# Middle attention layer: scores on and above the diagonal only, the other half transposed from their exponentials, edges multiplied in afterwards

## The reference

```python
A = jnp.concatenate([a_0, a_1, a_2, a_3], axis=1)
e = jnp.einsum('bid,bjd,dk->bkij', hidden, hidden, A)
e = jax.nn.leaky_relu(e, negative_slope=LEAKY_SLOPE)
scores = jnp.full_like(e[:, 0], NEG)
scores = jnp.where(adj == 1, e[:, 0], scores)
...
attn = jax.nn.softmax(scores, axis=-1)
return jnp.einsum('bij,bjd->bid', attn, hidden)
```

## Time and profile before

| | |
|---|---|
| median of 3 runs | 1610.05 us (1607.6 to 1613.08) |
| the profiled execution | 1606.74 us |
| its span, first to last instruction | 1604.9 us |
| first stages, until about | 440 us |
| attention stage | the rest |
| instructions | 32666 |

### The profile page before, as it was taken

The page is one execution under the profiler, slowest core; times in us unless marked ns, Lnnn a source line. Parts: engine busy times, 40 slices in busy tenths (PEclk is TensorE's granted clock), DMA queues, the critical chain, the costliest instruction groups (busy, mean ns, idle before and its releaser), DMA issues. The chain is left out here.

```text
span 1604.9 us, 32666 instructions
## 1 busy us (share of the span) xinstructions
PE 1465.7 (91%) x12740; PEld 1268.5 (79%) x12740; DVE 1137.0 (71%) x3198; ACT 921.2 (57%) x1825; POOL 203.2 (13%) x201
## 2 busy tenths in 40 slices
PE   3999998799836979999999999999999999999984
PEld 2999997555425859899898898988989889898774
DVE  3666664688635577887878878878788787886653
ACT  2777876122224666766657667566675766755620
POOL 4434430000000001011010111100111101010000
PEclk9999999799957989999999999999999999999996
DMA  9999991377811212213222132231322313212010
GB/s 189 207 209 213 210 210 67 110 244 244 288 39 47 79 47 69 76 47 99 54 85 81 39 106 76 57 93 28 112 74 54 93 35 105 67 34 61 28 35 25
DMA packets 108446, 161.94 MB, mean 101 GB/s; under 512 B 9344, under 2 KB 59136, under 8 KB 106240
## 3 DMA queue, kind: packets, MB, share of 16 engines
q1 hardware_dynamic: 85248, 117.86, 24.4%
q0 software_dynamic: 18432, 33.56, 11.4%
q10 hardware_dynamic: 4608, 8.39, 1.5%
HBM read 151.40 MB, written 41.94 MB: 120 GB/s over the span
## 5 line engine op out<-in xcount | busy, mean ns | idle before, releaser
L1329 PE MATMUL ps<-hV,wts_B 128*128 128x129 f32 x2048 | 246.2, 276 | 3.2 <-ACT wts_B L1128 3.0
L1329 PE MATMUL ps<-hP_A,wts_A 128*128 128x129 f32 x2048 | 239.0, 277 | 6.1 <-DVE wts_A L884 3.4
L1329 PE MATMUL ps<-hP_C,wts_C 128*128 128x129 f32 x2048 | 239.1, 277 | 6.0 <-DVE wts_C L884 6.0
L1329 PEld LDWEIGHTS ps<-hV,wts_B 128*128 128x128 f32 x2048 | 238.2, 192 | 4.6 <-ACT wts_B L1128 4.3
L1329 PEld LDWEIGHTS ps<-hP_A,wts_A 128*128 128x128 f32 x2048 | 234.4, 193 | 8.6 <-DVE wts_A L884 5.2
L1329 PEld LDWEIGHTS ps<-hP_C,wts_C 128*128 128x128 f32 x2048 | 234.3, 193 | 8.3 <-DVE wts_C L884 5.7
L889 DVE SCALAR_TENSOR_TENSOR wts_B<-wts_B 128x1024 f32<-128x1024 f32 x128 | 153.9, 1221 | 30.2 <-ACT wts_B L1124 30.2
L884 DVE SCALAR_TENSOR_TENSOR wts_A<-row_A,least_A,ring_A 128x1024 f32<-128x1024 f32 x128 | 161.2, 1275 | 9.2 <-ACT row_A L1108 8.3
L1124 ACT COPY wts_B<-ps 128x1024 f32<-128x1024 f32 x128 | 129.4, 1011 | 60.0 <-PE ps L1316 60.0
L884 DVE SCALAR_TENSOR_TENSOR wts_C<-row_C,least_C,ring_C 128x1024 f32<-128x1024 f32 x128 | 162.3, 1274 | 0.8 <-DMA ring_C<-maskT_scratch 0.8
L307 ACT ACTIVATE maskT<-ps 128x1024 fp8e4<-128x1024 bf16 x128 | 131.1, 1024 | 49.7 <-PE ps L341 37.7
(11 more groups left out here) (228 smaller groups left out, 2543.2 us busy)
## 6 DMA issues: line engine op xcount, KB each, us to landing
adj_b<-in_adj POOLq DMA_DIRECT2D x128, 256.0 KB, 9.1
maskT_scratch<-maskT SPq DMA_DIRECT2D x16, 1024.0 KB, 6.9
ring_A<-maskT_scratch SPq DMA_DIRECT2D x64, 256.0 KB, 3.3
off<-maskT_scratch SPq DMA_DIRECT2D x32, 512.0 KB, 6.7
ring_C<-maskT_scratch SPq DMA_DIRECT2D x64, 256.0 KB, 3.1
xa<-in_x SPq DMA_DIRECT2D x16, 512.0 KB, 4.3
whT_scratch<-whT_s ACTq DMA_DIRECT2D x32, 256.0 KB, 6.5
whT_b<-whT_scratch SPq DMA_DIRECT2D x16, 512.0 KB, 4.8
```

The lines of the kernel that those rows point to most:

```text
L1329: last = nc.tensor.matmul(Q_SLOTS[c // 2 % 2][:, c % 2, 0:PW], wts[x][:, j, c * P:c * P + P], src[:, j, :], start=(j == 0), stop=(j == T - 1))
```

## The change

The scores are symmetric, so tile row j is made only from its diagonal tile on (columns 128 j to 1023), without the penalty matmul. Keep, leaky and exponential work on that part alone. PE then transposes the 28 tiles above the diagonal of the exponentials into PSUM (`turn_rows`, 7 + 6 + ... + 1 tiles, in five groups placed between the columns of `weigh("A")`). `lower` on DVE multiplies the transposed tiles of row k by their edges and writes them below the diagonal, as column k of `wts["B"]`; `upper` on POOL multiplies the upper part of row k by its edges in place. The mask `off` is used as it is loaded, in its plain form, and `complement` is gone. `weigh("B")` waits for `up` and `low`. 

Around this, orders are rewritten: in the gram part C's `turn_h` comes first and the other C steps one place earlier; ACT takes two exponentials early and the other six after the last keep; `load_off` waits for `up` and `low` and stands behind the masks of C on SP, `save` behind `load_x`; the two elu steps of DVE move back. The turn i = B (16), which has no A, gets an order of its own: the transposes, then half of `weigh("C")`, all of `weigh("B")`, and the other half of `weigh("C")`.

```diff
-        PEN = 2048.0
...
-        pen_id = sb("pen_id", [P, P], bf16, side="right")
...
-        nc.vector.tensor_scalar(pen_id[:, :], ident[:, :], -PEN / EDGE_VALUE, None, ALU.mult)
...
+LT = T - 1
+GROUPS_T = ((0, 1), (1, 2), (2, 3), (3, 5), (5, 7))
+TURNED = [(1, 0), (0, 0), (1, 0), (0, 0), (0, HALF), (1, 0), (1, HALF)]
+def turned(k):
+    slot, at = TURNED[k]
+    return P_SLOTS[slot][:, at:at + (LT - k) * P]
...
         def load_off(b, h):
             if b > 0:
-                sp.wait_ge(S["B", "gram"], (b - 1) * T + 4 * h + 4)
+                sp.wait_ge(S["B", "up"], b * T)
+                sp.wait_ge(S["B", "low"], b * LT)
             sp.dma_start(off[:, 4 * h:4 * h + 4, :], maskT_dram[b, :, 4 * h:4 * h + 4, :]).then_inc(S["B", "ring"][h], 16)
...
-            if 0 <= i - 3:
-                save(i - 3)
             if 1 <= i + 1 < B:
                 load_mask("A", i + 1, 0)
                 load_mask("A", i + 1, 1)
-            if 0 < i < B:
-                load_off(i, 0)
-                load_off(i, 1)
             if 1 <= i + 2 < B:
                 load_q(i + 2)
             if 0 <= i - 2 < B:
                 load_mask("C", i - 2, 2)
                 load_mask("C", i - 2, 3)
+            if 0 < i < B:
+                load_off(i, 0)
+                load_off(i, 1)
             if 2 <= i + 2 < B:
                 load_x(i + 2)
+            if 0 <= i - 3:
+                save(i - 3)
             if 0 <= i - 1 < B:
                 load_mask("C", i - 1, 0)
                 load_mask("C", i - 1, 1)
...
+        def upper(b, k):
+            if k % 4 == 0:
+                pool.wait_ge(S["B", "ring"][k // 4], (b + 1) * 16)
+            if k < LT:
+                pool.wait_ge(S["B", "turned"], b * LT + k + 1)
+            else:
+                pool.wait_ge(S["B", "exps"], b * T + k + 1)
+            w = wts["B"][:, k, k * P:N]
+            pool.tensor_tensor(w, w, off_fp8[:, k, k * P:N], ALU.mult).then_inc(S["B", "up"], 1)
         for i in range(-1, B + 1):
+            if i >= 1:
+                upper(i - 1, 0)
+                upper(i - 1, 1)
             if i + 1 < B:
                 rstd("A", i + 1)
+            if i >= 1:
+                for k in range(2, T):
+                    upper(i - 1, k)
...
         def leaky(b, j):
             dve.wait_ge(S["B", "kept"], b * T + j + 1)
-            nc.vector.scalar_tensor_tensor(wts["B"][:, j, :], wts["B"][:, j, :], SLOPE, wts["B"][:, j, :], ALU.mult,
-                                           ALU.max).then_inc(S["B", "lrelu"], 1)
-        def complement(b, h):
-            dve.wait_ge(S["B", "ring"][h], (b + 1) * 16)
-            nc.vector.tensor_scalar(off_int[:, 4 * h:4 * h + 4, :], off_int[:, 4 * h:4 * h + 4, :], EDGES, None,
-                                    ALU.bitwise_xor).then_inc(S["B", "off"], 1)
+            w = wts["B"][:, j, j * P:N]
+            nc.vector.scalar_tensor_tensor(w, w, SLOPE, w, ALU.mult, ALU.max).then_inc(S["B", "lrelu"], 1)
+        def lower(b, k):
+            dve.wait_ge(S["B", "turned"], b * LT + k + 1)
+            if k == 0:
+                for h in range(2):
+                    dve.wait_ge(S["B", "ring"][h], (b + 1) * 16)
+            ks = slice(k * P, k * P + P)
+            nc.vector.tensor_tensor(wts["B"][:, k + 1:T, ks], turned(k).rearrange("p (t q) -> p t q", q=P),
+                                    off_fp8[:, k + 1:T, ks], ALU.mult).then_inc(S["B", "low"], 1)
...
+            def elu_positive():
+                dve.wait_ge(S["C", "quo"], (i - 2) * PARTS)
+                nc.vector.scalar_tensor_tensor(old[:, :, :], quo[:, :, :], 0.0, old[:, :, :], ALU.max, ALU.add)
+            def elu_negative():
+                dve.drain()
+                dve.wait_ge(S["C", "quo_exp"], i - 2)
+                nc.vector.scalar_tensor_tensor(old[:, :, :], elu[:, :, :], 1.0, old[:, :, :], ALU.min,
+                                               ALU.add).then_inc(S["C", "done"], 1)
...
@@ -937,30 +976,63 @@
                 leaky(i - 1, 0)
             if post:
                 highest_share("C", 2)
-                dve.wait_ge(S["C", "quo"], (i - 2) * PARTS)
-                nc.vector.scalar_tensor_tensor(old[:, :, :], quo[:, :, :], 0.0, old[:, :, :], ALU.max, ALU.add)
+            if post and not GW:
+                elu_positive()
             if GW:
                 leaky(i - 1, 1)
+            if CA:
+                columns("C", i - 2)
+            if GW:
                 leaky(i - 1, 2)
             if CA:
-                columns("C", i - 2)
+                exponents("C", i - 2)
             if GW:
                 leaky(i - 1, 3)
-            if CA:
-                exponents("C", i - 2)
-            if GW:
                 leaky(i - 1, 4)
             if CA:
                 factors("C", i - 2)
-            if post:
-                dve.drain()
-                dve.wait_ge(S["C", "quo_exp"], i - 2)
-                nc.vector.scalar_tensor_tensor(old[:, :, :], elu[:, :, :], 1.0, old[:, :, :], ALU.min,
-                                               ALU.add).then_inc(S["C", "done"], 1)
             if GW:
                 leaky(i - 1, 5)
                 leaky(i - 1, 6)
                 leaky(i - 1, 7)
+            if post and GW:
+                elu_positive()
+            if i == B:
+                lower(i - 1, 0)
+                weights("C", i - 2, 0)
+                weights("C", i - 2, 1)
+                lower(i - 1, 1)
+                weights("C", i - 2, 2)
+                lower(i - 1, 2)
+                weights("C", i - 2, 3)
+                lower(i - 1, 3)
+                lower(i - 1, 4)
+                elu_negative()
+                weights("C", i - 2, 4)
+                lower(i - 1, 5)
+                lower(i - 1, 6)
+                for j in range(5, T):
+                    weights("C", i - 2, j)
+                shares("C", i - 2, 0)
+                shares("C", i - 2, 1)
+                shares("B", i - 1, 0)
+                shares("B", i - 1, 1)
+                add("B", i - 1, 0, newC, oldC)
+                dve.drain()
+                stats("C", newC, 0)
+                shares("B", i - 1, 2)
+                shares("B", i - 1, 3)
+                highest_share("B", 1)
+                add("B", i - 1, 1, newC, oldC)
+                dve.drain()
+                stats("C", newC, 1)
+                moments("C")
+                shares("C", i - 2, 2)
+                shifts("C", i - 1)
+                return
...
                 dve.wait_ge(S["A", "qT_made"], i + 2)
                 nc.vector.tensor_tensor(newA[:, :, :], newA[:, :, :], TURN_Q.rearrange("p (t d) -> p t d", t=T),
                                         ALU.add).then_inc(S["A", "x1"], 1)
+            if GW:
+                lower(i - 1, 0)
+            if nextA:
                 dve.drain()
                 stats("A", newA, 0)
             if AA:
                 shares("A", i, 0)
+            if GW:
+                lower(i - 1, 1)
             if nextA:
                 stats("A", newA, 1)
                 moments("A")
             if AA:
                 shares("A", i, 1)
+            if GW:
+                lower(i - 1, 2)
             if CA:
                 weights("C", i - 2, 0)
+            if GW:
+                lower(i - 1, 3)
+                lower(i - 1, 4)
             if AA:
                 add("A", i, 0, newB, oldB)
             if nextA:
                 shifts("A", i + 1)
+            if AA:
+                shares("A", i, 2)
+            if GW:
+                lower(i - 1, 5)
+                lower(i - 1, 6)
+            if post and GW:
+                elu_negative()
             if CA:
                 weights("C", i - 2, 1)
-            if AA:
-                shares("A", i, 2)
-            if CA:
                 weights("C", i - 2, 2)
...
                 shares("B", i - 1, 3)
+            if post and not GW:
+                elu_negative()
...
             if j == 0 and b > 0:
                 act.wait_ge(S["B", "tile"], b * T)
-            nc.scalar.copy(wts["B"][:, j, :], P_SLOTS[j % 2]).then_inc(S["B", "kept"], 1)
+            nc.scalar.copy(wts["B"][:, j, j * P:N], P_SLOTS[j % 2][:, j * P:N]).then_inc(S["B", "kept"], 1)
         def score_exps(b, j):
             act.wait_ge(S["B", "lrelu"], b * T + j + 1)
-            nc.scalar.activation(wts["B"][:, j, :], wts["B"][:, j, :], ACT.Exp, bias=shiftB[:, 0:1]).then_inc(S["B", "exps"], 1)
+            w = wts["B"][:, j, j * P:N]
+            nc.scalar.activation(w, w, ACT.Exp, bias=shiftB[:, 0:1]).then_inc(S["B", "exps"], 1)
...
                 scaled("C", i - 3, 3)
+            if CA:
+                relu_hT("C", i - 2, "A", min(i + 1, B))
             if GW:
                 keep_scores(i - 1, 0)
                 keep_scores(i - 1, 1)
+                score_exps(i - 1, 0)
+                score_exps(i - 1, 1)
+                keep_scores(i - 1, 2)
+                keep_scores(i - 1, 3)
             if CA:
```

(94 more changed lines are left out.)

17 lines of the change are left out of this document (6 added, 11 removed).

## The result

The changed kernel takes 1616.29 us (median, 1611.93 to 1620.43), the kernel before beside it 1608.85. The ratio is 1.0045, 95% interval 1.0026 to 1.0063: slower, by about 7 us or 0.45%, where 1591 and a gain of 1% were forecast. The profiled execution took 1615.00 us, its span 1613.2 (1604.9 before).

What follows compares the result with a forecast made beforehand. PE was taken to bound the steady turn: -4.9 + 2.4 + 1.1 = -1.4 us, times 14 = -20; with -3.5 (i = 1) and +5 (end), 1606.7 became 1588, as median 1591; its own range 1578 to 1604, whole range 1560 to 1625.

Steps and rivals of the forecast that it cites:

- PE's sum and the gram chain: Steady turn: PE's own work 4.9 us shorter, 2.4 lost to a chain through the neighbours; gram part 12.0 us, not 17.45.
- rival (e): Narrow matmuls don't shorten as their columns say: together 0.3 us more a turn, inside the range; no chance of its own.
- The A part: Steady turn, PE: weighing 14.3, turn_q 0.87, transposes 3.05, together 18.2 us; the added waits all have cover over 1 us.
- GpSimd's rate: Upper steps on GpSimd: 2.2 ns a column, between bounds 1.45 and 2.9; 10.9 us a turn.
- The contention: Port pair shared by GpSimd and DVE: up 7 late for B's first column, 1.1 us a turn, bounds 0 and 1.9.
- Turn 16: Without an A part to cover the transposes, DVE's list ends at 30.2 and the last turn of C comes 6.2 us later.
- Turn 17: elu_negative leaves the way in front of weights C: -1.2 us.
- i = 1: Gram starts 1.9 us earlier, lasts some 10.6 us instead of 15.3, and transposes add 3.05: -3.5 us.
- (c): Slower by the port pair, GpSimd dear: at 2.9 ns a column up 7 is late, 1630 us; chance 0.27, including no change 0.10.
- (a): No contention: up 7 and shifts A in time, -2.5 us a turn, 1577 us; chance 0.19.
- (d): New waits drop PE's granted clock to 1.2 GHz for a while, adding 3 us a turn: 1633 us; chance 0.05.
- the four signs of being wrong: Gram part of 14 us, upper rows above 2.5 ns a column, granted clock under 0.95, last C turn not late.

## Why the prediction was wrong

**The sign.** -20 - 3.5 + 5 = -18.5 was forecast, the spans say +8.3.

**PE's sum and the gram chain: right.** 12.0 us, measured 12.11. The three stalls named were 0.9 for keep 2, 0.9 for `us_C` and 0.5 near the end; the trace has 0.18, 0.79 and 0.60, the last one on `hP_C` at A's first column, and one of 0.20 on `peak_C` that wasn't named. The chain is the one foreseen; that its sum came out to 0.1 is partly luck. Narrow matmuls cost as their columns say (three of 256 columns start within 0.33 us), so rival (e) is out.

**The A part: right.** 18.2 forecast, 18.38 measured, without a wait of PE in this turn.

**GpSimd's rate: right.** 2.2 ns a column was the middle between 1.45 and 2.9, and 1024 columns took 2.02 us, 2.0 ns a column. Up 7 ended at 938.57, 31.0 us behind the turn's start against 29.4 undisturbed and 33.7 with every claim served in turn. By PE's own pace B's first column reaches row 7 at about 939.6 (938.05 and 14 instructions of 0.112 us, an estimate), so it was in time. That the rate fell near the middle of so wide a pair of bounds is partly luck.

**The contention: right in kind, wrong in place and size; this is the step that failed.** The term is +1.1 us, for B's first column behind GpSimd, with nothing for the rest of the B part. Measured: 0 at the first column, +2.1 in the B part (20.03 against 17.94; up to 2.4 in three turns), nearly all at the values of the next A. The prediction costed GpSimd's own end. GpSimd did lose time (its six steps took 8.11 us, 6.5 forecast undisturbed), but it had cover. VectorE, which stood as well, had not: the earlier trace rows show GpSimd's power waiting for a weights step, and the reverse is now shown too. Beside the upper steps weights C 0 lost 0.82 us, `sf_A` 0.89, elu_negative 0.34, weights C 1 some 0.15. The Trainium skill states the rule for both directions (SBUF — State Buffer, section Who interferes with whom), and the trace now agrees: one small step of 8 columns took 0.94 us in the mean beside GpSimd. The prediction named that rule, and then followed it only to GpSimd's own end and to normed A, never down VectorE's queue.

**The B part taken as unchanged.** The steps -4.9 + 2.4 + 1.1 have no term for it. elu_negative was moved to 14 us later in the turn (29.2 us behind its start, 15.1 before), in front of shares A 3, A's last add and shares B 0; the prediction named it in the stretch of the upper steps and asked only if GpSimd would be served before it. It should have asked who is queued behind it on VectorE: 1.2 us of elu_negative and 2.2 of stretching, against the 1.99 us that VectorE had waited before shares A 3. In the B part the runs give 1.5 us back without GpSimd's upper steps and 1.2 with elu_negative out of the way. With the measured parts the steady turn is -5.3 (gram) + 3.2 (A) + 2.1 (B) = 0.0, where -1.4 was forecast.

**Turn 16: 6.2 forecast, 11.2 measured.** The list of VectorE steps was the right bound, but its weights C were costed at 1.2 us. Beside POOL the first four took 2.4, 2.4, 1.7 and 1.6, and stood before lower steps that held PE's PSUM slot: the list ended 33.2 us behind the turn's start instead of 30.2. Same cause, second place. From there to the end of C's first half PE took 7.4 us instead of 5.6, mostly because its granted clock was 0.50 from 1514.67, within the stall of 4.76 us, to 1531.73; the prediction had no term for that. The two make 4.8 of the 5.0 us. **Turn 17: -1.2 forecast, +0.9 measured.** elu_negative did leave the way, but the first weights of C then waited 1.0 us for their row terms (`row_C`), and PE waited for them nearly as long as before (2.21 against 2.40). The 0.9 lies behind the last weights: C's last 114 instructions took 14.99 us instead of 14.35, 4.2 us of them at a granted 0.50 and not 2.9, and the end test came 0.35 later. **i = 1: -3.5 forecast, -1.9 measured.** Its gram part shrank as forecast (15.3 to 10.9) and the transposes cost 3.1, but it started 0.6 us earlier and not 1.9. Turn 2 gave the other 1.8 of the 3.7 by turn 3 (67.50 to 65.71 us; -4.9 was forecast for the two), and that this comes near -3.5 is luck. It gained more than a steady turn since it has no elu_negative, and since its gram part had been 1.8 longer than a steady one's.

**The rivals.** (c), slower by the port pair, is the one that came, but by another way than it says: GpSimd wasn't dear, and up 7 wasn't late. (a), no contention, is about what the kernel without upper steps gives: 1592.6 measured, 1577 forecast, still 15 above. Some 12 of them lie in turns 2 to 15: a steady one takes 64.2 us where (a) has 63.25, and 0.6 of the difference is the B part, where elu_negative is still in the way. (d): the clock stayed at 1.00 in the steady turns and fell to 0.87 in turn 16, from 0.94. Of the four signs of being wrong, only a clock under 0.95 came, and in turn 16 alone; the length of the B part was not among them.

## What to carry to other kernels

When a step moves, list what is queued behind it on its own engine and when each of those is due, with the same care as for the step itself; a term of zero for a part of the turn needs its own line. When work goes to GpSimd, price every two-input SBUF step of VectorE beside it, the tiny ones too, and look whether a PSUM slot or a scale factor hangs on one of them; keep the rest of the port-heavy steps away from the stretch. Don't pull a step forward to where its engine must wait for the input: the work that stood in front of it filled that wait, and now has to be done after it.

## What the runs showed of the hardware

The stretching depends on the operands and on what is left of the other engine's step. The lower steps (one input in PSUM, one in SBUF) took 1.084 us for 896 columns both beside POOL and without it. DVE's steps with two SBUF inputs lost a little less than POOL's running step had left: weights C 0 started when POOL's step had 1.02 us to go and lost 0.82, `sf_A` with 1.03 to go lost 0.89 (128x8, 0.16 us alone), elu_negative with 0.48 lost 0.34, and A's add with 0.20 only 0.06. POOL's steps stood in the same way: the one of 640 columns, started 0.98 us after weights C 0, took 2.31 us, while 768 columns before it took 1.56.

A stall of 2.79 us cost 1.5 more behind it, since the granted clock fell to 0.50 as PE resumed. Shorter stalls mostly left it at 1.00: the eleven of 1.6 us and the one of 1.97 (turn 14) at the values in the changed kernel's steady turns did. But in the run with B's columns first, whose steady turns have the same order, the same stall in the same turn was followed by a fall:

```profile
1408.56 2.74 PE L1383 MATMUL ps<-w_use,hT_c 128*128 128x130 f32 x16 [1.97 <-ACT hT_c L1171]
1411.10 2.92 PE L1423 MATMUL ps<-hV,wts_B 128*128 128x129 f32 x16
```

The granted clock was 0.50 from 1409.70 to 1413.11, and that B part took 21.90 us instead of the 20.38 of the same turn in the changed kernel.
